# Swin block on one core: the copied values in two buffers in turn, unit 0's statistics ahead of other weights, and a new order of the pieces

## The chip, the cores and the metric

The kernel runs on one core of one Trainium2 chip. The metric is the device time of one execution in microseconds (us); the figure given for a kernel is the median of several executions.

## The reference, cut to what matters

The input `x` is [16, 192, 56, 56] in float32. One Swin block is computed on it and added to it:

```
xl  = layernorm(x over channels) * w + b, rolled by (-3, -3), cut in 7x7 windows (49 tokens each)
q, k, v = xw @ qkv_w.T + qkv_b                     # 6 heads of 32
out = softmax(q k^T / sqrt(32)) v, @ proj_w.T + proj_b
xl  = layernorm(out, windows put back and rolled back) * w + b
h   = gelu(xl @ fc1_w.T + fc1_b)                   # 768 wide
y   = h @ fc2_w.T + fc2_b + x
```

## The kernel before, in words

One unit of work is a row of 8 windows (7 image rows, 392 tokens). There are 16 x 8 = 128 units. Every large product is made in fp32r with operands split into a high and a low part: `five` and `five_tokens` issue five products where one would be enough for a coarser result.

Every engine has a program written out by hand, `step(t, k, it)`, run for t = 0 to 134. In a step an engine runs its pieces for several units at once; `units(t)` gives them, and `u[3]` is the unit t - 3. The order of the pieces inside `step` is fixed when the kernel is written, and each engine runs its pieces strictly in that order, each with its own semaphore waits. So an engine that waits in one piece holds up all pieces behind it.

A unit goes through these pieces:

- SyncE's queue (SP): `load_groups` (x in groups of 32 channels, for the statistics), `load` (x itself), `stats_out` (mean and 1/deviation to DRAM, L395), `stats_in` (them back, spread to all partitions, L402), `spread` (L434 to L442: the values `vs` copied into the block form `vbd`, 8 DMAs per unit, 4 for each half), `store`.
- VectorE (DVE): `token_blocks` (L933), `stats` and `mean_var` of the first norm, `less_mean` and `times_rstd` (L941, L945), `lo_part` (the low parts), `v_out` (L1042 to L1047, values from PSUM to `vs`, in two halves), `row_max`, `less_max`, `row_sum`, `row_scale` of the softmax, `stats`, `mean_var`, `normalise` of the second norm, `hidden_lo` (L1004), `finish_main` (L1009) and `finish_rest` (L1017).
- ScalarE (ACT): `hi_part` (the high parts), `q_out`, `k_out`, `q_rest_out`, `k_rest_out`, `exps`, `pt_copy` (transposed probabilities out of PSUM), `gelu_hi`, `gelu_full`, `y_low`.
- GpSimd (POOL): `rstd`, `less_mean_rest` (L1182), `times_rstd_rest` (L1186), `scaled_probs` (L1198), `hidden_lo_last`, `residual`.
- TensorE (PE): `qkv` (three tiles), `values` (four pieces; they make v), `scores`, `probs_t` (transposes), `weighted` (probabilities times values, 24 products that the trace shows as 48), `project`, `x2_channels`, `fc1` (six tiles), `fc2_hi` and `fc2_lo` (six each).

PSUM has 8 banks. `BANK_USES` says which bank each piece writes and in which order the uses of a bank follow each other; `claim` makes PE wait until the last reader of the use before is done. `fc2_hi(., 0)` claims the two banks of fc2, and so waits for `finish_main` and `finish_rest` of the unit before.

There is one buffer `vs` and one buffer `vbd`. `spread(u, .)` waits for `weighted(u - 1)`, which reads `vbd`:

```
sp.wait_ge(s_vs, nth(u, 2, c))
if u > 0:
    sp.wait_ge(s_pe["o"], nth(u - 1, 1, 0))
```

and `v_out(u, .)` waits until all 8 copies of unit u - 1 have landed, since they read `vs`. In DVE's order `v_out(u, 0)` stands ahead of `finish_rest`.

At the start, SP issues the x and weight loads of L387 to L430, then `load(0, 2)` to `load(0, 6)`, and only then enters its loop, whose first `stats_out` and `stats_in` belong to unit 0. PE makes the products for the folded bias of fc1 (L506, L507) before its first step. `less_mean(0)` on DVE is preceded by `first_weights` (scaling and splitting the qkv weights), and `lo_part("x1", 0, 1)` is followed by `other_weights`.

Of the kernel before, what the change touches and what calls it, by code (L numbers as in the profile page):

```python
# [56 lines left out]
REST = 16 * (6 + 4 + MT)  # L57
# [3 lines left out]
BANK_USES = [("o", 0, 2, 2), ("o", 1, 1, 2), ("qkv", 4, 7, 0), ("fc1", 0, 0, 3), ("vt", 0, 3, 0),  # L61
# [38 lines left out]
def swin_block_program(nc, x, n1w, n1b, qkv_wt, qkv_b, proj_wt, proj_b, n2w, n2b,  # L100
                       fc1_wt, fc1_b, fc2_wt, fc2_b, out):
    ctx = ExitStack()
    with ctx:
# [65 lines left out]
        vbd = sb("vbd", [128, 2, PAIRS, 3, WP])  # L169
        vs = sb("vs", [TP, PAIRS, C])  # L170
# [59 lines left out]
        s_vbd = sem("vbd_ready")  # L230
# [141 lines left out]
        def _(sp):  # L372
# [50 lines left out]
            for vec, cols in ((n2w, 4), (n2b, 6)):  # L423
                norm_vector(sp, vec, cols, s_rest)
# [7 lines left out]
            def spread(u, c):  # L432

                sp.wait_ge(s_vs, nth(u, 2, c))  # L434
                if u > 0:
                    sp.wait_ge(s_pe["o"], nth(u - 1, 1, 0))
                src = vs[:, 2 * c:2 * c + 2, :].rearrange("p j (a e d) -> p (j a) e d", a=3, e=2)
                dst = vbd[:, :, 2 * c:2 * c + 2, :, :].rearrange("p i j a d -> p i (j a) d")
                for wi in range(2):
                    for e in range(2):  # L440
                        sp.dma_start(dst[WP * e:WP * e + N, wi, :, DH * e:DH * e + DH],  # L441
                                     src[N * wi:N * wi + N, :, e, :]).then_inc(s_vbd, 16)  # L442

            for i in range(2, AHEAD):
                load(0, i)
            for t in range(UNITS + 7):
                if t < UNITS:
                    if t > 1:
                        load_groups(t)
                if 0 <= t - 2 < UNITS:  # L450
                    stats_in(t - 2)
                if 0 <= t - 4 < UNITS:
                    spread(t - 4, 0)
                    spread(t - 4, 1)
                if 0 <= t - 1 < UNITS:
                    stats_out(t - 1)
# [18 lines left out]
        def _(pe):  # L475
# [26 lines left out]
            pe.wait_ge(s_rest, REST)  # L502
            pe.wait_ge(s_raw[2], 16 * 3)
            for m in range(MT):
                ps = psum[:, spare_1, m:m + 1]
                nc.tensor.matmul(ps, raw_1[0][:, m * 128:(m + 1) * 128], nwb[:, 6:7], start=True, stop=False)  # L506
                last = nc.tensor.matmul(ps, raw_1[1][0:CR, m * 128:(m + 1) * 128], nwb[0:CR, 7:8], start=False, stop=True)  # L507
            last.then_inc(s_bias_mm, 1)
            pe.wait_ge(s_zero, 1)
            pe.wait_ge(s_zero_qk, 4)  # L510
            pe.wait_ge(s_split, 1)

# [63 lines left out]
            def weighted(u, j):  # L576
                if j == 0:
                    claim(u, [("o", 0), ("o", 1)], (s_vbd, VMOVES, VMOVES - 1), (s_ptc, PAIRS, 0))
# [4 lines left out]
                for wi, p in ((0, 0), (0, 1), (1, 0), (1, 1), (0, 2), (1, 2)):  # L583
# [7 lines left out]
                    last = nc.tensor.matmul(ps, vbd[0:KP, wi, j, p, :], pt[:, j, block, N * side:N * side + N],  # L591
# [18 lines left out]
            def step(t, k, it):  # L610
                u = units(t)
                if u[2] is not None:
                    weighted(u[2], 0)
                    weighted(u[2], 1)
                    weighted(u[2], 2)
                    weighted(u[2], 3)
                if u[4] is not None:
                    fc2_lo(u[4], 3)
                    fc2_hi(u[4], 4)
                    fc2_hi(u[4], 5)  # L620
                    fc2_lo(u[4], 4)
                if u[0] is not None:
                    qkv(u[0], 4)
                if u[4] is not None:
                    fc2_lo(u[4], 5)
                if u[3] is not None:
                    fc1(u[3], 0)
                if u[0] is not None:
                    values(u[0], 0)
                    values(u[0], 1)  # L630
                if u[3] is not None:
                    fc1(u[3], 1)
                if u[2] is not None:
                    project(u[2], 0)
                if u[3] is not None:
                    fc1(u[3], 2)
                if u[2] is not None:
                    project(u[2], 1)
                    project(u[2], 2)
                    project(u[2], 3)  # L640
                if u[3] is not None:
                    fc2_hi(u[3], 0)
                    fc2_hi(u[3], 1)
                if u[0] is not None:
                    qkv(u[0], 3)
                if u[3] is not None:
# [606 lines left out]
```

## Time and profile before

| | |
|---|---|
| median of 3 runs | 3142.04 us (3140.3 to 3142.78) |
| the profiled execution | 3141.32 us |
| its span, first to last instruction | 3139.5 us |
| PE busy | 2916.0 us (93%) |
| ACT busy | 2679.8 us (85%) |
| DVE busy | 2641.6 us (84%) |
| POOL busy | 1298.8 us (41%) |
| granted TensorE clock, mean | 0.996 |

Busy time of an engine is the time in which at least one of its instructions runs. The shares are averages over the whole span, and what bounds a stretch is read from the waits in it. The chain of waits follows what ended last backwards, step by step, to what released it.

### The profile page before, as it was taken

To read this page: it belongs to the slowest core of one execution; us is meant where nothing else is said; L and a number is where in the kernel's file an instruction comes from. 1 tells how busy PE (TensorE), PEld (TensorE's weight loads), DVE (VectorE), ACT (ScalarE), POOL (GpSimd) and SP (SyncE) were. 2 spreads that over 40 slices of the span, in tenths; PEclk is the share of its full clock that TensorE was granted. 3 is DMA by queue.
4 is the path that set the end of the run, shared out by engine and by line. 5 is a ranking of instruction groups with operands and counts; after the bars stand their busy time and mean duration, and the time that the engine had idled before them with its cause. 6 is when DMAs were issued, how large, how long until landed. Compare 5 with 4: busy or idle time off the path is not lost.

```text
span 3139.5 us, 74916 instructions
## 1 busy us (share of the span) xinstructions
PE 2916.0 (93%) x26284; PEld 2826.4 (90%) x26284; DVE 2641.6 (84%) x7212; ACT 2679.8 (85%) x5500; POOL 1298.8 (41%) x1548
## 2 busy tenths in 40 slices
PE   3899999999999999999999999999999999999998
PEld 2899999999999999999999999999998999999998
DVE  5888888888888888888888888888888888888885
ACT  1788888888888888888888888888888888888886
POOL 1444444434444444344444434434443443444442
PEclk9999999999999999999999999999999999999999
DMA  4222322333232233323323323332322333233221
GB/s 96 55 66 67 76 66 65 75 68 67 68 75 66 65 71 72 67 67 75 67 65 73 70 65 71 72 67 67 76 66 64 71 72 66 66 72 71 65 55 28
DMA packets 606164, 213.11 MB, mean 68 GB/s; under 512 B 461411, under 2 KB 589156, under 8 KB 605796
## 3 DMA queue, kind: packets, MB, share of 16 engines
q1 hardware_dynamic: 602468, 206.64, 29.4%
q8 instruction: 217, 3.56, 0.5%
q10 hardware_dynamic: 3328, 1.68, 0.2%
q14 instruction: 151, 1.24, 0.1%
HBM read 130.69 MB, written 38.94 MB: 54 GB/s over the span
## 4 chain that ended last, share of the span: by engine, by line
PE 57%; SPq 24%; DMA 9%; DVE 5%; issue 4%; ACT 0%; POOL 0%; POOLq 0%; ACTq 0%
SPq L441 23%; DMA vbd<-vs 9%; PE psum L591 6%; PE psum L566 6%; PE psum L572 4%; PE psum L546 4%; PE psum L317 4%; PE psum L319 4%; PE psum L318 4%; PE psum L320 4%; PE psum L321 4%; PE psum L547 3%; PE psum L548 3%; PE psum L567 3%; PE psum L557 2%
## 5 line engine op out<-in xcount | busy, mean ns | idle before, releaser
L1198 POOL TENSOR_TENSOR pr<-pr,rc 98x294 f32<-98x294 f32 x512 | 346.7, 686 | 1103.2 <-DVE rc L1040 1103.2
L742 ACT ACTIVATE hh<-psum,b 128x392 fp32r<-128x392 f32 x768 | 450.5, 587 | 47.8 <-PE psum L558 23.7
L745 ACT ACTIVATE hf<-psum,b 128x392 f32<-128x392 f32 x768 | 445.8, 581 | 6.3
L546 PE MATMUL psum<-hh,w2h 128*128 128x392 f32 x768 | 274.6, 358 | 153.1 <-DVE yr L1017 153.1
L1047 DVE COPY vs<-psum 98x384 f32<-98x384 f32 x256 | 142.8, 558 | 319.4 <-DMA vbd<-vs 263.1
L1004 DVE TENSOR_TENSOR hl<-hf,hh 128x392 fp32r<-128x392 f32 x640 | 399.0, 624 | 10.8 <-ACT hf L745 10.8
L1171 POOL TENSOR_TENSOR ve<-mv,eps 98x4 f32<-98x4 f32 x256 | 80.3, 314 | 590.1 <-DVE mv L962 590.1
L546 PEld LDWEIGHTS psum<-hh,w2h 128*128 128x128 f32 x768 | 144.4, 188 | 176.2 <-issue 170.4
L967 DVE TENSOR_SCALAR xn<-psum,mv,rs 98x192 f32<-98x192 f32 x512 | 230.0, 469 | 78.1 <-POOL rs L1175 78.1
L557 PE MATMUL psum<-hl,w2h 128*128 128x392 f32 x768 | 275.0, 358 | 0.0
L780 ACT ACTIVATE km<-psum,bk,half_k 128x392 f32<-128x392 f32 x256 | 160.2, 677 | 134.4 <-PE psum L321 134.4
L317 PE MATMUL psum<-x_h,w_mh 128*128 128x392 f32 x768 | 268.7, 350 | 0.5 <-DVE o_l L993 0.5
L547 PE MATMUL psum<-hh,w2l 128*128 128x392 f32 x768 | 262.6, 342 | 0.0
L319 PE MATMUL psum<-x_l,w_mh 128*128 128x392 f32 x768 | 262.0, 341 | 0.0
L548 PE MATMUL psum<-hh,w2r 128*128 128x392 f32 x768 | 261.6, 341 | 0.0
L318 PE MATMUL psum<-x_h,w_ml 128*128 128x392 f32 x768 | 261.4, 340 | 0.0
L566 PE MATMUL psum<-km,qm 128*98 128x98 f32 x2048 | 261.0, 249 | 0.0
L558 PE MATMUL psum<-hl,w2h 128*64 128x392 f32 x768 | 260.9, 340 | 0.0
L320 PE MATMUL psum<-x_r,w_rh 128*128 128x392 f32 x768 | 260.7, 339 | 0.0
L321 PE MATMUL psum<-x_r,w_rl 128*128 128x392 f32 x768 | 259.5, 338 | 0.0
L1027 DVE TENSOR_REDUCE mx<-psum 98x6 f32<-98x294 f32 x512 | 233.6, 456 | 10.9 <-PE psum L567 0.6
L1032 DVE TENSOR_TENSOR pr<-psum,mx 98x294 f32<-98x294 f32 x512 | 234.5, 458 | 4.2
(144 smaller groups left out, 10467.4 us busy)
## 6 DMA issues: line engine op xcount, KB each, us to landing
bc<-mean_rstd SPq DMA_DIRECT2D x128, 392.0 KB, 3.6
vbd<-vs SPq DMA_DIRECT2D x1024, 36.8 KB
xg<-in_x SPq DMA_DIRECT2D x368, 96.0 KB, 2.4
xt<-in_x SPq DMA_DIRECT2D x112, 194.5 KB, 2.7
out<-xt SPq DMA_DIRECT2D x112, 194.5 KB, 1.9
xt<-in_x SPq DMA_DIRECT2D x112, 97.2 KB, 2.5
out<-xt SPq DMA_DIRECT2D x112, 97.2 KB, 2.1
xg<-in_x SPq DMA_DIRECT2D x128, 3.8 KB, 2.0
```

The costliest lines, as they stand in the source:

```text
L317: nc.tensor.matmul(ps, wmh[:, c0:c0 + m], xh, start=True, stop=False)
L318: nc.tensor.matmul(ps, wml[:, c0:c0 + m], xh, start=False, stop=False)
L319: nc.tensor.matmul(ps, wmh[:, c0:c0 + m], xl, start=False, stop=False)
L320: nc.tensor.matmul(ps, wrh[:, c0:c0 + m], xrr, start=False, stop=False)
L321: return nc.tensor.matmul(ps, wrl[:, c0:c0 + m], xrr, start=False, stop=True)
L441: sp.dma_start(dst[WP * e:WP * e + N, wi, :, DH * e:DH * e + DH], src[N * wi:N * wi + N, :, e, :]).then_inc(s_vbd, 16)
L546: nc.tensor.matmul(ym, w2h[:, m, 0:CM], hh[:, b, :], start=a, stop=False)
L547: nc.tensor.matmul(ym, w2l[:, m, :], hh[:, b, :], start=False, stop=False)
L566: nc.tensor.matmul(ps[:, TP * wi:TP * wi + TP], qm[:, w, :], km[:, w, :], start=True, stop=True)
L742: nc.scalar.activation(hh[:, m % HB, :], bank("fc1", m)[:, 0:T], ACT.Gelu, bias=b1[:, m:m + 1]).then_inc(s_hh, 1)
L745: nc.scalar.activation(hf[:, m % HB, :], bank("fc1", m)[:, 0:T], ACT.Gelu, bias=b1[:, m:m + 1]).then_inc(s_gelu, 1)
L1004: nc.vector.tensor_tensor(hl[:, b, :], hf[:, b, :], hh[:, b, :].bitcast(F32), ALU.subtract).then_inc(s_hl, 1)
```

## The change

1. `vs` and `vbd` get a second copy, used by unit parity, and `s_vbd` becomes two semaphores. `spread(u, .)` now waits for `weighted(u - 2)`, and `v_out(u, .)` for the copies of unit u - 2. PE's wait for `vbd` counts on the semaphore of its parity.
2. SP's order. In the prologue: `stats_out(0)` and `stats_in(0)` stand behind `load_groups(1)`, then come `load_groups(2)`, `load(0, 1)` and the other weights; `load(0, 2)` to `load(0, 6)` move into the loop, one per step. In the loop the second half of a unit's spread is issued one step behind its first half, and ahead of the next unit's first half.
3. The vectors of the second norm are loaded from ACT's queue (semaphore `s_n2`). The products of fc1's bias move from ahead of PE's first step to behind `qkv(0, 4)`, and DVE adds them at the end of `other_weights`. The memset of `vbd` moves from DVE to POOL.
4. `BANK_USES` is new, and so is the order in every engine's `step`.

```
-        vbd = sb("vbd", [128, 2, PAIRS, 3, WP])
-        vs = sb("vs", [TP, PAIRS, C])
+        vbd = sb("vbd", [128, 2, 2, PAIRS, 3, WP])
+        vs = sb("vs", [TP, 2, PAIRS, C])
...
             load_groups(0)
-            load(0, 0)
             for at, c0, m in qkv_columns():
                 sp.dma_start(raw_q[0][:, at:at + m], qkv_wt[0:CM, c0:c0 + m]).then_inc(s_raw[0], 16)
+            load(0, 0)
             load_groups(1)
+            stats_out(0)
+            stats_in(0)
+            load_groups(2)
             load(0, 1)
...
                 sp.wait_ge(s_vs, nth(u, 2, c))
-                if u > 0:
-                    sp.wait_ge(s_pe["o"], nth(u - 1, 1, 0))
+                if u > 1:
+
+                    sp.wait_ge(s_pe["o"], nth(u - 2, 1, 0))
...
-            for i in range(2, AHEAD):
-                load(0, i)
             for t in range(UNITS + 7):
                 if t < UNITS:
-                    if t > 1:
+                    if t > 2:
                         load_groups(t)
+                    if 1 < t < AHEAD:
+                        load(0, t)
                 if 0 <= t - 2 < UNITS:
-                    stats_in(t - 2)
+                    if t - 2 > 0:
+                        stats_in(t - 2)
                 if 0 <= t - 4 < UNITS:
-                    spread(t - 4, 0)
                     spread(t - 4, 1)
+                if 0 <= t - 3 < UNITS:
+                    spread(t - 3, 0)
                 if 0 <= t - 1 < UNITS:
-                    stats_out(t - 1)
+                    if t - 1 > 0:
+                        stats_out(t - 1)
...
             def v_out(u, c):
-                if not (isinstance(u, int) and u == 0):
-
-                    dve.wait_ge(s_vbd, nth(u - 1, VMOVES, VMOVES - 1))
+                if u > 1:
+
+                    dve.wait_ge(s_vbd[u % 2], nth(u // 2 - 1, VMOVES, VMOVES - 1))
...
+BANK_USES = [("vt", 0, 5, 0), ("qkv", 4, 7, 0), ("vt", 1, 6, 0), ("fc1", 0, 4, 3), ("fc1", 1, 1, 3),
+             ("qkv", 3, 2, 0), ("ln2", 0, 6, 2), ("ln2", 1, 0, 2), ("fc1", 2, 5, 3), ("pt", 0, 1, 1),
+             ("qkv", 2, 4, 0), ("fc1", 3, 7, 3), ("fc2", 0, 1, 3), ("fc2", 1, 3, 3), ("fc1", 4, 2, 3),
+             ("fc1", 5, 5, 3), ("s", 0, 6, 0), ("pt", 1, 7, 1), ("pt", 2, 4, 1), ("s", 1, 0, 0),
+             ("x2", 0, 2, 2), ("s", 2, 7, 0), ("x2", 1, 6, 2), ("pt", 3, 5, 1), ("s", 3, 4, 0),
+             ("o", 0, 2, 1), ("o", 1, 0, 1)]
```

The new orders, written with u for the unit of which PE makes q, k and v in its step (the other engines' step numbers are translated to PE's; a bare number is the piece's index):

- PE: values u 0; fc2_lo u-4 3; qkv u 4; fc2_lo u-4 4, 5; values u 1, 2; fc1 u-3 0; values u 3; fc1 u-3 1; qkv u 3; project u-2 0, 1, 2; fc1 u-3 2; project u-2 3; probs_t u-1 0; qkv u 2; fc1 u-3 3; fc2_hi u-3 0, 1; fc2_lo u-3 0; fc2_hi u-3 2; fc1 u-3 4; fc2_lo u-3 1, 2; fc1 u-3 5; fc2_hi u-3 3; scores u 0; probs_t u-1 1, 2; scores u 1; x2_channels u-2 0; fc2_hi u-3 4, 5; scores u 2; x2_channels u-2 1; probs_t u-1 3; scores u 3; weighted u-1 0 to 3.
- ACT: gelu_full u-4 4; gelu_hi u-4 5; pt_copy u-2 1; hi x1 u 1; pt_copy u-2 2; hi x2 u-3 0; gelu_full u-4 5; exps u-1 0; pt_copy u-2 3; hi x2 u-3 1; exps u-1 1; hi o u-2 0; exps u-1 2; hi o u-2 1; q_rest u; exps u-1 3; gelu_hi u-3 0; y_low u-4; gelu_full u-3 0; gelu_hi u-3 1; k_rest u 0; gelu_full u-3 1; k_rest u 1; k_out u 0; pt_copy u-1 0; k_out u 1; gelu_hi and gelu_full u-3 2; q_out u 0; gelu_hi and gelu_full u-3 3; q_out u 1; hi x1 u+1 0; gelu_hi u-3 4.
- DVE: less_max u-1 2; row_sum u-1 0; mean_var first norm u+2 0; row_max u-1 3; row_sum u-1 1; row_scale u-1 0; mean_var u+2 1; x2_rest_lo u-3; mean_var u+2 2; less_max u-1 3; lo o u-2; finish_main u-4; mean_var u+2 3; v_out u 0; o_rest_lo u-2; v_out u 1; token_blocks u+3; stats second norm u-2 0; stats first norm u+3 0; finish_rest u-4; stats u-2 1; row_sum u-1 2; stats u-2 2; less_mean u+1; hidden_lo u-3 0; stats u-2 3; row_scale u-1 1; mean_var u-2 0 to 2; row_scale u-1 2; mean_var u-2 3; times_rstd u+1; hidden_lo u-3 1, 2; stats u+3 1; row_sum u-1 3; normalise u-2 0, 1; stats u+3 2; normalise u-2 2, 3; row_scale u-1 3; lo x1 u+1 0; row_max u 0; hidden_lo u-3 3; less_max u 0; row_max u 1; lo x2 u-2 0; less_max u 1; hidden_lo u-3 4; lo x1 u+1 1; row_max u 2; stats u+3 3.
- POOL: scaled_probs u-2 3; hidden_lo_last u-4; scaled_probs u-1 0; rstd first norm u+2; less_mean_rest and times_rstd_rest u+1; rstd second norm u-2; scaled_probs u-1 1; residual u-4; scaled_probs u-1 2.

## Rows read from the trace of the kernel before

**Rows 1.** The page: busy time of the engines, and shares of the chain.
```profile
PE 2916.0 (93%) x26284; PEld 2826.4 (90%) x26284; DVE 2641.6 (84%) x7212; ACT 2679.8 (85%) x5500; POOL 1298.8 (41%) x1548
...
PE 57%; SPq 24%; DMA 9%; DVE 5%; issue 4%; ACT 0%; POOL 0%; POOLq 0%; ACTq 0%
```

**Rows 2.** Waits, 200 to 3000 us: total us, times, longest.
```profile
DVE vs L1047 <- DMA vbd<-vs: 236.0, 117, 4.0
...
PE psum L546 <- DVE yr L1017: 144.4, 117, 3.2
```

**Rows 3.** Chain of waits in order of time: start, us, what.
```profile
1490.46 1.56 PE psum L591 x48
1492.08 0.88 SPq L441
...
1498.02 2.22 DMA vbd<-vs
...
1501.75 0.42 PE psum L546
```

**Rows 4.** Single lines of DVE, 200 to 2900 us: min/median/max ns, first and last start.
```profile
L945 DVE TENSOR_TENSOR ym<-ym,bc x113: 511/518/524, 216.7 to 2887.1; 128x392 f32<-128x392 f32 x113
...
L1004 DVE TENSOR_TENSOR hl<-hf,hh x566: 526/557/1241, 202.4 to 2896.5; 128x392 fp32r<-128x392 f32 x189
```

**Rows 5.** Busy time of one period: length, PE, PEld, DVE, ACT, POOL.
```profile
1490.39:1514.08 23.69, 22.57 (x207) 21.90 (x206) 20.44 (x57) 21.00 (x44) 10.13 (x12) 1.00 0.34 78
```

**Rows 6.** Timeline of PE in that period: start, duration, what.
```profile
1498.13 0.25 PE L331 MATMUL psum<-wp_rl,o_b 128*98 128x192 f32 x1
1498.22 0.36 PE L317 MATMUL psum<-x_h,w_mh 128*128 128x392 f32 x1
1498.42 0.34 PE L318 MATMUL psum<-x_h,w_ml 128*128 128x392 f32 x1
1498.60 0.34 PE L319 MATMUL psum<-x_l,w_mh 128*128 128x392 f32 x1
...
1512.96 0.51 PE L566 MATMUL psum<-km,qm 128*98 128x98 f32 x4
...
1513.48 0.50 PE L530 MATMUL psum<-ident,xn 98*128 98x98 f32 x4
...
1514.08 1.61 PE L591 MATMUL psum<-pt,vbd 113*64 113x49 f32 x48
1515.61 0.45 PE L557 MATMUL psum<-hl,w2h 128*128 128x392 f32 x1
1515.90 0.34 PE L558 MATMUL psum<-hl,w2h 128*64 128x392 f32 x1
```

**Rows 7.** Timeline of the first 100 us, SP, POOL, DVE and PE.
```profile
9.49 3.20 SPq L387 DMA_DIRECT2D xg<-in_x  x5
...
38.19 0.57 SPq L395 DMA_DIRECT2D mean_rstd<-mv  x1
...
12.09 1.03 POOL L1175 TENSOR_TENSOR mv<-ve,half 98x4 f32<-98x4 f32 x1
...
42.59 1.53 DVE L933 STREAM_TRANSPOSE xtok<-xg 128x768 f32<-128x768 f32 x1 [2.36 <-DMA xg<-in_x]
44.06 0.37 DVE L898 MEMSET half_k<- 32x1 f32 x4
...
49.89 0.56 DVE L941 TENSOR_TENSOR ym<-xt,bc 128x392 f32<-128x392 f32 x1
...
53.54 0.67 PE L317 MATMUL psum<-x_h,wq_mh 128*128 128x392 f32 x1 [18.86 <-DVE x_r L996]
...
96.36 0.42 PE L317 MATMUL psum<-x_h,wq_mh 128*128 128x392 f32 x1 [3.25 <-DVE vs L1047]
```

**Rows 8.** Timeline of SP in one period, its first store to `stats_in`.
```profile
1504.27 0.38 SPq L409 DMA_DIRECT2D out<-xt  x1
...
1511.77 0.62 SPq L402 DMA_DIRECT2D bc<-mean_rstd  x1
```

More of the change, by code:

```diff
@@ L611, in step @@
                 u = units(t)
[L612 to L616, printed above, removed]
+                if u[0] is not None:
+                    values(u[0], 0)
                 if u[4] is not None:
                     fc2_lo(u[4], 3)
-                    fc2_hi(u[4], 4)
-                    fc2_hi(u[4], 5)
-                    fc2_lo(u[4], 4)
                 if u[0] is not None:
@@ L624, in step @@
                 if u[4] is not None:
+                    fc2_lo(u[4], 4)
                     fc2_lo(u[4], 5)
+                if u[0] is not None:
+                    values(u[0], 1)
+                    values(u[0], 2)
                 if u[3] is not None:
@@ L637, in step @@
                 if u[2] is not None:
-                    project(u[2], 1)
-                    project(u[2], 2)
                     project(u[2], 3)
[L641 to L646, printed above, removed]
-                    fc2_lo(u[3], 0)
-                    fc1(u[3], 3)
-                    fc2_hi(u[3], 2)
+                if u[1] is not None:
+                    probs_t(u[1], 0)
                 if u[0] is not None:
@@ L652, in step @@
                 if u[3] is not None:
+                    fc1(u[3], 3)
+                    fc2_hi(u[3], 0)
+                    fc2_hi(u[3], 1)
+                    fc2_lo(u[3], 0)
+                    fc2_hi(u[3], 2)
                     fc1(u[3], 4)
@@ L670, in step @@
                     scores(u[0], 1)
+                if u[2] is not None:
+                    x2_channels(u[2], 0)
+                if u[3] is not None:
+                    fc2_hi(u[3], 4)
+                    fc2_hi(u[3], 5)
+                if u[0] is not None:
+                    scores(u[0], 2)
+                if u[2] is not None:
+                    x2_channels(u[2], 1)
                 if u[1] is not None:
@@ L796, in step @@
                 u = units(t)
+                if u[5] is not None:
+                    gelu_full(u[5], 4)
+                    gelu_hi(u[5], 5)
+                if u[3] is not None:
+                    pt_copy(u[3], 1)
+                if u[1] is not None:
+                    hi_part("x1", u[1], 1)
+                if u[3] is not None:
+                    pt_copy(u[3], 2)
+                if u[4] is not None:
+                    hi_part("x2", u[4], 0)
+                if u[5] is not None:
+                    gelu_full(u[5], 5)
@@ new lines, in step @@
+                if u[1] is not None:
+                    q_rest_out(u[1])
+                if u[2] is not None:
+                    exps(u[2], 3)
+                if u[4] is not None:
+                    gelu_hi(u[4], 0)
+                if u[5] is not None:
+                    y_low(u[5])
+                if u[4] is not None:
+                    gelu_full(u[4], 0)
+                    gelu_hi(u[4], 1)
+                if u[1] is not None:
+                    k_rest_out(u[1], 0)
+                if u[4] is not None:
+                    gelu_full(u[4], 1)
@@ new lines, in step @@
+                if u[1] is not None:
+                    k_rest_out(u[1], 1)
+                    k_out(u[1], 0)
+                if u[2] is not None:
+                    pt_copy(u[2], 0)
+                if u[1] is not None:
+                    k_out(u[1], 1)
+                if u[4] is not None:
+                    gelu_hi(u[4], 2)
+                    gelu_full(u[4], 2)
+                if u[1] is not None:
+                    q_out(u[1], 0)
+                if u[4] is not None:
+                    gelu_hi(u[4], 3)
+                    gelu_full(u[4], 3)
@@ L851, in step @@
-                if u[0] is not None:
-                    q_out(u[0], 1)
-                if u[3] is not None:
-                    gelu_full(u[3], 4)
-                    gelu_hi(u[3], 5)
+                    gelu_hi(u[4], 4)
             steps(step)
@@ L1057, in step @@
                 if u[5] is not None:
[L1058 to L1067 removed]
+                    stats(1, u[5], 0)
                 if u[0] is not None:
@@ L1071, in step @@
                     finish_rest(u[7])
+                if u[5] is not None:
+                    stats(1, u[5], 1)
+                if u[4] is not None:
+                    row_sum(u[4], 2)
+                if u[5] is not None:
+                    stats(1, u[5], 2)
+                if u[2] is not None:
+                    less_mean(u[2], (k - 2) % SLOTS)
                 if u[6] is not None:
@@ L1127, in step @@
                     row_max(u[3], 0)
-                if u[0] is not None:
-                    mean_var(0, u[0], 0)
+                if u[6] is not None:
+                    hidden_lo(u[6], 3)
                 if u[3] is not None:
```

269 lines of the change are left out of this document (113 added, 156 removed), and 5 rows, old and new, of the table BANK_USES.

## The prediction

> **What bounds the kernel now.** I read the busy shares first: PE 93%, ACT 85%, DVE 84% [rows 1]. PE leads, but 7% of the span is not PE's, and the chain of waits gives PE only 57% of the span and SP's queue 24% [rows 1]. The waits of the steady part name the place: `fc2_hi(., 0)` waits for DVE's `finish_rest` once per unit, 144.4 us in 117 times, or 1.23 us each; DVE's `v_out` waits for the copies of the unit before, 236.0 us in 117 times [rows 2]. The chain in order of time shows how the two hang together [rows 3]: `weighted` from 1490.46, the first of 8 SP copies at 1492.08, the last copy's transfer from 1498.02 for 2.22 us, then `v_out` and `finish_rest` on DVE, and PE's product at 1501.75. That is a loop: from the start of `weighted` to the stalled product 11.3 us, and from there 12.3 us of PE work to the next `weighted` (1514.08, [rows 6]).
>
> The period is 23.84 us: the first and last start of L945, 113 units, give (2887.1 - 216.7) / 112 [rows 4]. Without the stall it is 23.84 - 1.23 = 22.61 us, which agrees with PE's 22.57 us busy in one period of 23.69 us. In that period ACT is busy for 21.00 us and DVE for 20.44 us, POOL for 10.13 us [rows 5]. So a period cannot go below about 22.6 us while PE's work stays, and ACT would then be at 93%, DVE at 90%.
>
> **1. Two buffers in turn.** `spread(u)` waits for `weighted(u - 2)`, and `v_out(u)` for copies issued a whole period before. SP's 8 issues and the transfer leave the loop. SP itself stays far from full: 6.7 us of copies (the transfer of the last starts 5.9 us behind the first issue, [rows 3], and each takes 0.8) and 8.1 us from its first store to the end of `stats_in` [rows 8], in 22.6 us. What it gives, if nothing else is late: 1.23 us per unit, 144.4 us in the 117 units of [rows 2] and about 4 us in the others, 148 us in all.
>
> **2. What is late next: the new order, laid out by hand.** I place PE's pieces one after the other from the start of `values(u, 0)` = 0, at the spacing of [rows 6]: 0.178 us for a product of 392 columns (1498.42 to 1498.60), 0.09 for one of 192 (1498.13 to 1498.22), 0.52 for a scores piece (1512.96 to 1513.48), 1.53 for `weighted` (1514.08 to 1515.61). Multiplied out: 75 x 0.178 + 40 x 0.09 + 4 x 0.52 + 1.53 + 1.6 for 18 transposes = 22.2 us; the other 0.4 us of the busy 22.57 lies where the form changes. Ends of pieces: `fc2_lo 5` 2.4, `values 1` 2.9, `values 3` 4.6, `fc1 1` 5.5, `project 1` 7.3, `project 3` 9.1, `qkv 2` 10.2, `fc2_lo 0` 12.6, `fc1 5` 15.6, `scores 0` 16.6, `scores 2` 19.6, `scores 3` 20.6, `weighted` 22.2.
>
> Against these I place the other engines in their own order, each piece at the spacing of the same period, 0.15 us for each hand-over. DVE: it waits for `fc2_lo 5` until 2.55 in `finish_main`, then `v_out 0` ends at 3.7, `v_out 1` at 5.4, `token_blocks` 6.9, waits for `project 1` until 7.5, `finish_rest` 8.5, `hidden_lo 0` 10.5, `hidden_lo 2` 12.8, `normalise 3` 15.3, waits for `scores 0` until 16.8, `lo x1 1` 20.6, `row_max 2` 21.0, and back at `finish_main` after 3.5 us of pieces, at 2.3 of the next period. The layout closes on itself with 1.8 us of idle DVE time. ACT: `gelu_hi 5` and `gelu_full 4` end at 16.4, it waits for `probs_t 1` until 17.0, the table load and `exps 0` end at 20.8, `pt_copy 3` 21.2, `hi o` 2.3 (next period), `gelu_hi 0` 5.3, `gelu_full 1` 8.1, `pt_copy 0` 9.9, `gelu_hi 3` 13.2 after 0.6 us of waiting for `fc2_lo 0`, `gelu_hi 4` 15.4: it closes with 1.1 to 1.6 us idle. POOL reaches `scaled_probs 1` at 13.5 and `scaled_probs 3` at 16.1.
>
> PE's waits, each with the time it has left: `values(u, 0)` for `lo x1` 1.9 us; `project 0` for `o_rest_lo` (4.5) 1.9; its bank for `v_out 1` 1.0; `fc2_hi 0` for `finish_rest` (8.5) 2.6 and, since bank 1 is now shared, for `pt_copy 0` 1.2; `probs_t 0` for `gelu_full 1` 1.0; `probs_t 3` for `gelu_full 5` (19.2) 0.7; `weighted`'s bank for `lo x2` 1.5 and for `less_max 1` 1.1; `weighted 3` for `pt_copy 3` 0.5. None is negative. A schedule that closes at 22.6 us with all waits met means that no loop of waits is longer, so PE again has no gap. The least cover is 0.5 us, so a single queue running a little later than laid out shows. I charge 0.1 us per unit for this, 12 us (between 0 and 0.5 us, 0 to 62 us).
>
> **3. Changes of form on PE.** One from 192 to 392 columns costs 0.02 us (1498.22 to 1498.42 against 0.18), the one after `weighted` 0.11 (1515.61 to 1515.90) [rows 6]. Before there were five, at 0.19 us together; in the new order there are seven (four of the first kind, two from transposes to 392 columns, one from `weighted` to 192), for which these two rows give 0.12 to 0.41 us. The difference is -0.07 to +0.22 us per unit, -9 to +28 us; I take +6 us, near the cheap row, because five of the seven are like or near it.
>
> **4. Unit 0's statistics ahead.** Before, `stats_out(0)` is issued at 38.19 us though its data were ready at 13.1 [rows 7]. Now it follows `load_groups(1)`, which ends at 12.7 (9.49 + 3.20, and the same issues lie ahead of it). DVE is there sooner, one memset of 1.3 us less. Then 2 us to land, `stats_in`, and the three groups of unit 2 from 15.5 to 18.1 with 2.5 us to land. DVE takes `token_blocks(2)` (1.5 us) ahead of the weights, so `first_weights` starts at about 22.5 in place of 44.06, ends 5.8 us later (44.06 to 49.89) at 28.3, and PE's first product of unit 0 comes 3.65 us behind (49.89 to 53.54), at 32.0 in place of 53.54 [rows 7]: -21.5 us (between -14, if the groups of unit 2 or bc come late behind the weight loads, and -25). The products of fc1's bias, 6.2 us, now lie inside unit 0's step. DVE spends 9 us in `other_weights` at that time and PE has nothing that could pass it, so they cost nothing; uncovered they would cost 6.2. The vectors on ACT's queue end at about 21 us, ahead of ACT's first work at 28, and are free.
>
> **5. First units and the end.** Between 57 and 100 us PE waits for the same copies, 3.25 us once at 96.36 [rows 7], and other waits there are for chains of latencies that stay. I take -6 us (0 to -12). The last seven steps have the same pieces: 0 +- 3.
>
> The sum against the profiled execution: 3141.3 - 148 + 12 + 6 - 21.5 - 6 = 2983.8 us. The median shown is 0.7 us above it, so 2984 us is forecast for the median too.
>
> **A rule against the change.** L1004 takes 557 ns in the median but up to 1241 [rows 4], so some DVE operations with two SBUF inputs already stand behind a GpSimd one. The Trainium skill (SBUF - State Buffer, "SBUF: two separate sides") says that such a DVE operation and a GpSimd operation hold one port pair exclusively, whichever starts first, for its whole length. By this rule the trace's spread is a matter of who meets whom, and the new order decides it anew; it is the second rival.
>
> **Rivals.**
> A. Another engine becomes the bound. ACT and DVE have only 1.1 to 1.8 us of idle time in the layout, and each engine's waits add if they fall at other places: ACT's 21.00 us plus the 2.0 us of waits laid out gives 23.0 us, DVE's 20.44 + 0.35 + 1.8 = 22.6. At 23.2 us per unit the steady part gives only 0.64 x 120 = 77 us: 3141 - 77 - 27 + 6 = 3043 us. For it: three engines over 90% on strict queues. Against it: the waits in the layout are waits for PE, which shrink when an engine runs late. 14%.
> B. The copies' wait goes but PE's stays: the loop closes over `finish_main`, `finish_rest` and the bank shared with `pt_copy 0`, or over SP's strict order (`store(u-4)` waits for `residual` at 14.5, and `stats_in` and both spreads queue behind it). Then only the start is won: 3141 - 27 = 3114 us. Against it: SP is through with the spreads at 7.1 of the next period, 13 us before `weighted`. 5%.
> C. Slower: DVE and POOL collide. Nine DVE operations per unit read two SBUF operands (five `hidden_lo`, `less_mean`, `times_rstd`, two `lo x1`), and a collision costs up to 1241 - 557 = 0.68 us. DVE has 23.84 - 20.44 - 0.35 = 3.05 us to the old period, so from five collisions more per unit on, the kernel is slower. At seven more, DVE's period is 20.8 + 4.8 = 25.6 us: 3141 + 1.75 x 120 - 27 = 3324 us; at five, about 3160. Against it: POOL is busy for 10.1 of 22.6 us, most of it laid out beside `token_blocks`, `stats` and `normalise`. 3%.
> The change doing what it says with the waits gone has 78%.
>
> **How the numbers follow.** The likeliest case by itself reaches from 3141 - 148 - 9 - 25 - 12 = 2947 to 2984 + 50 (0.5 us per unit in place of 0.1) = 3034 us, most of it between 2955 and 3020. The range is drawn down to 2948 and up to 3050, which takes in rival A. What this measurement can tell from no change is 0.2%, about 6 us. Faster: the likeliest case, A, and all but a little of B, 0.94; within 0.2%: 0.02; slower: C and what I have not seen, 0.04.
>
> **What would show it.** Right: the wait of `v_out` for `vbd<-vs` and of L546 for `yr` gone from the waits; PE over 97% busy from 200 to 2900 us at a period of 22.6 to 22.8; the first product of unit 0 near 32 us; DVE idle in `finish_main` and before the second norm's statistics, waiting for PE. Wrong: a new wait of PE once per unit (for `pt`, `gelu_full` or `lo x1`), PE busy for more than 22.9 us per unit (step 3), L1004's mean well above 0.62 us (rival C), or `stats_out(0)` later than 15 us (step 4).

## The result and the profile after

The changed kernel takes 2939.93 us (median of 4 runs, 2938.56 to 2941.19) against 3141.17 us of the kernel before, timed beside it (3137.77 to 3142.78): a ratio of 0.9361, 95% interval 0.9344 to 0.9377. The forecast was 2984 us, in the range 2948 to 3050. The direction and the place of the gain came out as forecast; the gain is 44 us larger, and the time lies 8 us below the lower end of the range. The profiled execution took 2939.99 us, with a span of 2938.2 us and a granted clock of 0.999.

The page of the changed kernel: busy time of the engines, and the shares of the chain that ended last (against [rows 1]).

```profile
PE 2888.9 (98%) x26284; PEld 2820.7 (96%) x26284; DVE 2692.8 (92%) x7211; ACT 2689.2 (92%) x5500; POOL 1365.5 (46%) x1549
...
PE 97%; DVE 1%; ACT 1%; SPq 0%; DMA 0%; issue 0%; POOL 0%; POOLq 0%; ACTq 0%
```

SP's queue and the transfers, together a third of the chain before, are off it: the chain is PE's own work. PE's busy time also fell, by 27.1 us, with the same 26,284 products. It is the first sign of where the missing 44 us lie: if busy time were work alone, the same products would have the same busy time.

Its waits from 200 to 2900 us (total us, times, longest; against [rows 2]):

```profile
DVE mx L1046 <- PE psum L575: 122.8, 120, 2.2
...
ACT pt L713 <- PE psum L580: 62.6, 121, 0.7
...
ACT hh L756 <- PE psum L566: 32.4, 122, 1.0
...
PE psum L318 <- DVE pr L1051: 0.6, 1, 0.6
...
PE psum L580 <- ACT hf L759: 0.2, 1, 0.2
```

Both waits of [rows 2] are gone. What waits now is DVE, for the scores (1.02 us per unit; 0.8 was laid out), and ACT, for `probs_t` (0.52; 0.6 laid out) and `fc2_lo 0` (0.27; 0.6 laid out): all for PE. DVE also waits 0.21 us per unit for ACT's high part. The two other waits of DVE that were laid out, in `finish_main` and ahead of the second norm's statistics, did not come (7.6 us in 8 times in all). PE itself waits for nobody, two single waits in 120 units aside. The windows say the same (length, then busy time of PE, PEld, DVE, ACT and POOL, granted clock, DMA share, GB/s; the second is one period, against [rows 5]):

```profile
200.00:2900.00 2700.00, 2699.19 (x24658) 2639.22 (x24657) 2505.48 (x6717) 2531.56 (x5172) 1276.07 (x1440) 1.00 0.32 72
...
1517.98:1540.40 22.42, 22.42 (x207) 21.93 (x205) 20.89 (x57) 21.04 (x44) 10.65 (x13) 1.00 0.32 73
```

Single lines of DVE, min/median/max ns, first and last start (against [rows 4]):

```profile
L964 DVE TENSOR_TENSOR ym<-ym,bc x119: 532/533/539, 208.5 to 2853.5; 128x392 f32<-128x392 f32 x119
...
L1023 DVE TENSOR_TENSOR hl<-hf,hh x604: 528/558/568, 207.2 to 2899.0; 128x392 fp32r<-128x392 f32 x151
```

119 units give a period of (2853.5 - 208.5) / 118 = 22.415 us, against 23.842 before. The starts of `weighted` divide the whole difference of the spans, 3139.5 - 2938.2 = 201.3 us. First the kernel before, then the changed one, the fourth and the last but one of each:

```profile
154.86 1.61 PE L591 MATMUL psum<-pt,vbd 113*64 113x49 f32 x48
...
3086.17 1.61 PE L591 MATMUL psum<-pt,vbd 113*64 113x49 f32 x48
```

```profile
128.24 1.61 PE L600 MATMUL psum<-pt,vbd 113*64 113x49 f32 x48
...
2885.36 1.61 PE L600 MATMUL psum<-pt,vbd 113*64 113x49 f32 x48
```

Up to the first of these lie 26.6 us (154.86 - 128.24), in the 123 periods between them 123 x 1.416 = 174.2 us, and behind the last 0.5 us. The start (timeline, SP, DVE and PE; against [rows 7]):

```profile
12.74 0.47 SPq L396 DMA_DIRECT2D mean_rstd<-mv  x1
...
14.97 0.35 SPq L403 DMA_DIRECT2D bc<-mean_rstd  x1
15.36 2.73 SPq L388 DMA_DIRECT2D xg<-in_x  x5
...
25.89 1.53 DVE L952 STREAM_TRANSPOSE xtok<-xg 128x768 f32<-128x768 f32 x1 [8.18 <-DMA xg<-in_x]
...
32.07 0.56 DVE L960 TENSOR_TENSOR ym<-xt,bc 128x392 f32<-128x392 f32 x1
...
35.16 0.45 PE L328 MATMUL psum<-wq_mh,x_h 128*98 128x192 f32 x1 [16.33 <-DVE x_r L1015]
```

### The profile page after: what moved, and what is told of

Its sections match the earlier page's. It is cut to its first block, busy times and chain, and to the rows that moved or that the text cites. A ratio compares the mean times of both kernels' runs of the same rounds, so it can differ in the third digit from the quotient of the medians.

```text
span 2938.2 us, 75046 instructions
## 1 busy us (share of the span) xinstructions
PE 2888.9 (98%) x26284; PEld 2820.7 (96%) x26284; DVE 2692.8 (92%) x7211; ACT 2689.2 (92%) x5500; POOL 1365.5 (46%) x1549
## 4 chain that ended last, share of the span: by engine, by line
PE 97%; DVE 1%; ACT 1%; SPq 0%; DMA 0%; issue 0%; POOL 0%; POOLq 0%; ACTq 0%
PE psum L318 8%; PE psum L319 7%; PE psum L320 7%; PE psum L322 7%; PE psum L321 7%; PE psum L600 7%; PE psum L574 6%; PE psum L554 5%; PE psum L565 5%; PE psum L555 5%; PE psum L566 5%; PE psum L556 5%; PE psum L580 4%; PE psum L328 4%; PE psum L330 3%; PE psum L329 3%
## 5 line engine op out<-in xcount | busy, mean ns | idle before, releaser
L1215 POOL TENSOR_TENSOR pr<-pr,rc 98x294 f32<-98x294 f32 x512 | 385.9, 764 | 382.3 <-DVE rc L1059 382.3
L759 ACT ACTIVATE hf<-psum,b 128x392 f32<-128x392 f32 x768 | 451.7, 588 | 6.3
L1209 POOL TENSOR_TENSOR hl<-hf,hh 128x392 fp32r<-128x392 f32 x128 | 226.0, 1766 | 374.3 <-ACT hf L759 374.3
L1023 DVE TENSOR_TENSOR hl<-hf,hh 128x392 fp32r<-128x392 f32 x640 | 347.7, 559 | 3.8 <-ACT hf L759 3.7
L318 PE MATMUL psum<-x_h,w_mh 128*128 128x392 f32 x768 | 275.0, 358 | 0.7 <-DVE pr L1051 0.6
L713 ACT ACTIVATE pt<-psum 113x294 f32<-113x294 f32 x512 | 207.1, 405 | 70.4 <-PE psum L580 70.2
L565 PE MATMUL psum<-hl,w2h 128*128 128x392 f32 x768 | 264.5, 344 | 0.3 <-POOL hl L1209 0.3
L574 PEld LDWEIGHTS psum<-km,qm 128*98 128x98 f32 x2048 | 237.0, 166 | 11.3 <-ACT qm L716 4.6
L768 ACT ACTIVATE pr<-pr 98x294 f32<-98x294 f32 x512 | 230.2, 450 | 7.7 <-DVE pr L1051 3.1
```

The source lines that it names most:

```text
L318: nc.tensor.matmul(ps, wmh[:, c0:c0 + m], xh, start=True, stop=False)
L565: nc.tensor.matmul(ym, w2h[:, m, 0:CM], hl[:, b, :], start=False, stop=z)
L574: nc.tensor.matmul(ps[:, TP * wi:TP * wi + TP], qm[:, w, :], km[:, w, :], start=True, stop=True)
L759: nc.scalar.activation(hf[:, m % HB, :], bank("fc1", m)[:, 0:T], ACT.Gelu, bias=b1[:, m:m + 1]).then_inc(s_gelu, 1)
```

## The experiments

The first three ask where the missing gain lies. Theory 1: a wait of PE costs more than the idle time that the profile labels with it. The last product ahead of it counts as busy to its end, and in a stream without a wait that tail lies under the next products; behind the wait the first products follow each other more slowly. So PE's real floor lies below the 22.57 us of [rows 5], and taking the stall away gives more than 1.23 us. Theory 2: the stall is worth 1.23 us, and PE's work became cheaper through the new order. The other experiments take the parts of the change apart.

**One part alone: the two buffers, in the order before.**

```
-        vbd = sb("vbd", [128, 2, PAIRS, 3, WP])
-        vs = sb("vs", [TP, PAIRS, C])
+        vbd = sb("vbd", [128, 2, 2, PAIRS, 3, WP])
+        vs = sb("vs", [TP, 2, PAIRS, C])
...
-                if u > 0:
-                    sp.wait_ge(s_pe["o"], nth(u - 1, 1, 0))
+                if u > 1:
+                    sp.wait_ge(s_pe["o"], nth(u - 2, 1, 0))
...
```

> The kernel before with the two buffers alone (vs and vbd by parity, two semaphores); the order of every queue and the banks stay as before. Theory 1 (a stall of PE costs more than its labelled idle time, because the product before it drains and the one behind it refills the pipeline: 0.16 + 0.08 us per stall): the waits of v_out for the copies and of fc2_hi for finish_rest vanish and the period falls from 23.84 to about 22.4 us, 2965 to 2975 us in all. Theory 2 (a stall costs its idle time of 1.23 us, and the rest of the gain is the new order's cheaper changes of form on PE): the waits vanish but the period stays at 22.6 us, 2988 to 2996 us. Theory 3 (the new order was needed to remove the wait): a wait of PE stays each unit, above 3030 us.

Measured: 2953.45 us (2951.82 to 2954.46), ratio 0.9403 (0.9389 to 0.9417). The line that paces DVE, PE's window and DVE's wait:

```profile
L946 DVE TENSOR_TENSOR ym<-ym,bc x112: 511/516/523, 315.6 to 2798.6; 128x392 f32<-128x392 f32 x112
```

```profile
300.00:2800.00 2500.00, 2500.00 (x22927) 2438.61 (x22925) 2297.26 (x6263) 2333.71 (x4808) 1139.21 (x1339) 1.00 0.32 74
```

```profile
DVE vs L1047 <- PE psum L331: 92.1, 95, 1.0
```

The period is (2798.6 - 315.6) / 111 = 22.369 us, without a gap on PE. This is the old order, so theory 2 is out: the stall by itself was worth 23.842 - 22.369 = 1.473 us per unit, and the new order's period is 0.046 us longer than this. PE's busy time over the run fell from 2916.0 to 2883.8 us, with the same number of products. The time is also some 12 us below the lower end that theory 1 gave, mostly because the fill became shorter as well: the fourth `weighted` starts at 147.19 us instead of 154.86, 7.7 us sooner, with the first product of unit 0 where it was (53.64).

**A wait with next to nothing in it.** PE waits for its own last product once per unit, behind `fc2_lo 5`:

```
                     fc2_lo(u[4], 5)
+                    pe.wait_ge(s_pe["fc2"], nth(u[4], MT, MT - 1))
```

> The kernel after with one wait added per unit: behind fc2_lo(u-4, 5) PE waits for that product itself before it goes on to values(u, 1). Nothing is late; PE only may not overlap two products at this place. Theory 1: the hidden cost of a stall shows by itself, drain and refill, 0.2 to 0.35 us per unit, of which only 0.0 to 0.1 us is labelled as idle: 2965 to 2985 us. Theory 2: what a wait costs is its labelled idle time: below 0.1 us per unit, 2940 to 2952 us.

Measured: 2976.42 us (2975.8 to 2977.01), ratio 0.9476 (0.946 to 0.9492). DVE's pacing line, PE's window, and PE's timeline at the place:

```profile
L965 DVE TENSOR_TENSOR ym<-ym,bc x111: 532/536/539, 302.7 to 2799.0; 128x392 f32<-128x392 f32 x111
```

```profile
300.00:2800.00 2500.00, 2493.66 (x22577) 2404.89 (x22576) 2314.34 (x6176) 2318.48 (x4738) 1172.87 (x1322) 1.00 0.32 73
```

```profile
1518.74 0.33 PE L566 MATMUL psum<-hl,w2h 128*64 128x392 f32 x1
...
1519.14 0.33 PE L328 MATMUL psum<-wq_mh,x_h 128*98 128x192 f32 x1
1519.31 0.25 PE L329 MATMUL psum<-wq_ml,x_h 128*98 128x192 f32 x1
```

The same three products in the changed kernel without the wait:

```profile
1521.88 0.33 PE L566 MATMUL psum<-hl,w2h 128*64 128x392 f32 x1
1522.05 0.25 PE L328 MATMUL psum<-wq_mh,x_h 128*98 128x192 f32 x1
1522.13 0.25 PE L329 MATMUL psum<-wq_ml,x_h 128*98 128x192 f32 x1
```

The period is (2799.0 - 302.7) / 110 = 22.694 us, 0.279 more than without the wait, and the window counts as idle only (2500 - 2493.66) / 110 = 0.058 us of it. The timeline shows the rest: the next product comes 0.40 us behind the last one instead of 0.17 (1519.14 - 1518.74 against 1522.05 - 1521.88), but 0.33 us of the 0.40 count as busy. The one behind it comes after 0.17 instead of 0.08. Together 0.23 + 0.09 = 0.32 us, close to the 0.279.

What the slow restart is, PE's weight loads show (PEld), first in the changed kernel, then behind the wait:

```profile
1521.88 0.16 PEld L328 LDWEIGHTS psum<-wq_mh,x_h 128*98 128x98 f32 x1
```

```profile
1519.13 0.16 PEld L328 LDWEIGHTS psum<-wq_mh,x_h 128*98 128x98 f32 x1 [0.43 <-PE psum L566]
1519.22 0.17 PEld L329 LDWEIGHTS psum<-wq_ml,x_h 128*98 128x98 f32 x1
```

In the stream a product's weights are loaded 0.17 us ahead of it, under the product before (1521.88 for 1522.05). Behind the wait the first load starts together with its product (1519.13 and 1519.14), and the second product follows its own load, which starts 0.09 us later. So the wait also takes away the lead of the weight loads.

**Four such waits** (also behind `values 1`, `qkv 3` and `project 1`).

```
+                    pe.wait_ge(s_pe["vt"], nth(u[0], 2, 0))
...
+                    pe.wait_ge(s_pe["qkv"], nth(u[0], 3, 1))
...
+                    pe.wait_ge(s_pe["ln2"], nth(u[2], 2, 0))
```

> The kernel after with four waits of PE for its own last product per unit: behind fc2_lo(u-4, 5), values(u, 1), qkv(u, 3) and project(u-2, 1). One such wait cost 36.5 us in all, 0.28 us per unit, 0.06 of it labelled idle. Theory 1 (each place where products may not overlap costs about the same, drain and refill): 3 more times 0.2 to 0.28 us per unit, period 23.3 to 23.55 us, 3050 to 3085 us. Theory 2 (the first wait cost its 0.28 because it moved other engines into PE's way): much less than proportional, below 3020 us.

Measured: 3086.74 us (3086.0 to 3087.31), ratio 0.9834 (0.9819 to 0.9849).

```profile
L968 DVE TENSOR_TENSOR ym<-ym,bc x106: 532/535/539, 309.9 to 2786.5; 128x392 f32<-128x392 f32 x106
```

```profile
300.00:2800.00 2500.00, 2475.68 (x21730) 2321.25 (x21730) 2223.62 (x5936) 2242.66 (x4559) 1126.94 (x1272) 1.00 0.31 70
```

The period is (2786.5 - 309.9) / 105 = 23.587 us: 1.172 more, 0.293 for each wait, of which 0.058 is counted as idle (24.3 us in some 105 units, by four). The period and the time lie just above the upper ends of theory 1 (23.55 us and 3085 us), so the cost adds up, by a little more than in proportion. Four waits for nothing cost four fifths of what the removed stall cost, with a fifth of its labelled idle time.

**The new order with one buffer.** The inverse of the first edit on the changed kernel, and both halves of the copies issued together, as before:

```
+                    spread(t - 4, 0)
                     spread(t - 4, 1)
...
-                if 0 <= t - 3 < UNITS:
-                    spread(t - 3, 0)
```

> The kernel after with one buffer of vs and vbd and both halves of the spread issued together as before; all else as after. Theory: the loop comes back and the new order makes it worse, since v_out(u, 0) waits for copies that start with the period: 8 issues and a landing end at 8.9 us, v_out 1 about 5.7 us later than laid out, and project 0 shares its bank: 4 to 5 us of PE stall per unit, 3450 to 3550 us. Rival (the order alone gives the gain, the buffers little): within 50 us of the kernel after, below 2990 us.

Measured: 3866.11 us (3864.3 to 3870.85), ratio 1.2312 (1.2293 to 1.233), granted clock 0.903. The waits, and PE behind one of them:

```profile
DVE vs L1065 <- DMA vbd<-vs: 435.6, 84, 6.9
PE psum L328 <- DVE vs L1065: 421.5, 84, 6.8
```

```profile
1503.74 0.30 PE L328 MATMUL psum<-wp_mh,o_h 128*98 128x192 f32 x1 [4.15 <-DVE vs L1065]
...
1506.36 0.53 PE L319 MATMUL psum<-x_h,w_ml 128*128 128x392 f32 x1
1506.69 0.53 PE L320 MATMUL psum<-x_l,w_mh 128*128 128x392 f32 x1
```

```profile
1500.00:1510.00 10.00, 6.26 (x38) 6.27 (x39) 6.93 (x17) 4.61 (x11) 0.71 (x1) 0.83 0.05 7
```

The loop of [rows 3] is back, and dearer: PE waits 421.5 / 84 = 5.0 us per unit (300 to 2800 us), as the expectation had it. Its reason, that the new order asks for `v_out` earlier behind `weighted`, was not tested apart. The time was missed by over 300 us, because the expectation knew only the wait. Behind it the products of 392 columns last 0.53 us and follow each other after 0.33, about half the speed of the other runs. The granted clock is at its lower level of 1.2 GHz there: PE had stood still for 4.15 us up to 1503.74, the clock's mean is 0.53 from 1504 to 1506 us and 0.61 from 1506 to 1508, and from 1508 on it is 1.00 again (0.83 in the mean of these 10 us). The period is 29.84 us, 7.4 more than with two buffers. How the 2.4 us that are not labelled wait divide was not measured apart; if such a stall hides 0.24 us, as the one of the kernel before does, some 2.1 us are the clock's, an estimate.

**The start put back** (SP's prologue as before, the rest as changed).

```
-            stats_out(0)
-            stats_in(0)
-            load_groups(2)
...
+            for i in range(2, AHEAD):
+                load(0, i)
```

> The kernel after with SP's prologue as before: stats_out(0) and stats_in(0) in the loop, behind load(0, 2) to load(0, 6). Theory: the start term is real and not given back: first product of unit 0 about 18 us later, 2956 to 2963 us in all. Rival (the delay is absorbed in the fill, since units 1 to 3 wait for chains of latencies anyway): less than 10 us, below 2950 us.

Measured: 2957.38 us (2957.31 to 2957.94), ratio 0.9417 (0.9402 to 0.9431): 17.5 us slower than the changed kernel.

```profile
50.47 0.45 PE L328 MATMUL psum<-wq_mh,x_h 128*98 128x192 f32 x1 [31.71 <-DVE x_r L1010]
```

PE starts 50.47 - 35.16 = 15.3 us later, not 18, and 17.5 us are lost, 16.3 of them ahead of the fourth `weighted` (144.56 against 128.24). The start is a term of its own.

**Both terms without the new order** (two buffers and the new start, PE's, DVE's and ACT's order and the banks as before).

> The kernel before with the two buffers and the new start (SP's prologue, second-norm vectors on ACT's queue, fc1's bias products behind qkv(0, 4), vbd's memset on POOL), but the old banks, the old order of pieces and both halves of the spread together. Theory (the two terms add, and the new order is worth nothing or costs 5 us): 2953 less 18, 2933 to 2938 us, so a little below the kernel after (2940). Rival (the new order is needed for the early start, since the old one has v_out and token_blocks of later units in the way of unit 0): 2945 us or more.

Measured: 2935.86 us (2934.87 to 2937.61), ratio 0.9354 (0.934 to 0.9368), 17.6 us below the buffers alone. The terms add: the fourth `weighted` starts at 129.01 us, 18.2 sooner than with the buffers alone. The new order of the pieces gave nothing: the changed kernel's 2939.93 us lie 4 us above, in line with its longer period (0.046 x 123 = 5.7 us).

**The order of one piece.** `lo_part("x1", u[2], 1)` moved behind `row_max(u[3], 2)` and `stats(0, u[0], 3)`, away from POOL's `hidden_lo_last`.

> The kernel after with DVE's lo_part(x1, u+1, 1) moved behind row_max(u, 2) and stats(u+3, 3), away from POOL's hidden_lo_last. Theory (the two have two SBUF inputs and block each other; it costs DVE and POOL time but not the kernel's): the DVE piece falls from 1283 to about 560 ns and POOL's from 1777 to 1030 to 1300 ns, total within 3 us of the kernel after. Rival (the long durations have another cause, such as operands waiting in the engine): both stay above 1200 ns. A PE wait at values(u, 0) would show that the 1.9 us of cover laid out there were needed.

Measured: 2939.18 us (2938.41 to 2940.3), ratio 0.9364 (0.935 to 0.938). The groups from 200 us on (busy us, mean ns | idle before), first in the changed kernel, then here:

```profile
L1015 DVE TENSOR_TENSOR x_r<-yr,x_r 64x392 fp32r<-64x392 f32 x119 | 152.6, 1283 | 3.8
...
L1209 POOL TENSOR_TENSOR hl<-hf,hh 128x392 fp32r<-128x392 f32 x120 | 213.2, 1777 | 349.5 <-ACT hf L759 349.5
```

```profile
L1015 DVE TENSOR_TENSOR x_r<-yr,x_r 64x392 fp32r<-64x392 f32 x119 | 76.1, 639 | 3.7
...
L1209 POOL TENSOR_TENSOR hl<-hf,hh 128x392 fp32r<-128x392 f32 x120 | 212.4, 1770 | 348.6 <-ACT hf L759 348.6
```

DVE's collision costs 0.64 us per unit and can be taken away, and nothing follows, since DVE has 1.02 us of waiting for PE. POOL's operation, which I had expected to fall as well, stays as long. The edit took only one of two DVE operations away from it: `hidden_lo`, which has two SBUF operands as well, starts 0.33 us behind POOL's operation in both versions (1516.96 and 1516.63 there, 1517.47 and 1517.14 here). So what was moved is not what lengthens it; `hidden_lo` may be, and was not tested.

**PE's first product sooner.** In front of DVE's step 2, on the version with the old order (`b_best`), there with `stats_out(1)` behind `load(0, 1)` as well (`b_best2`), and on the changed kernel (`a_first`):

```
+                if t == 2:
+                    less_mean(0, 0)
+                    times_rstd(0)
...
-                if u[2] is not None:
+                if u[2] is not None and t > 2:
                     less_mean(u[2], (k - 2) % SLOTS)
...
```

`b_best` is this edit alone on the old order:

> As b_two_stats, and in DVE's step 2 first_weights, less_mean(0) and times_rstd(0) stand at the front, ahead of token_blocks(2), where DVE idles for 8.2 us in the kernel after (17.7 to 25.9 us). Theory: unit 0's x1 is ready 5 to 7 us sooner and all of it reaches the end, 2926 to 2931 us. Rival (the other weights and the loads for them become the bound of the fill): less than 3 us below b_two_stats.

`b_best2` adds the earlier `stats_out(1)`, since DVE stood 3.59 us for it in `b_best`:

> The old order with two buffers, the new start, the pieces of unit 0 at the front of DVE's step 2, and stats_out(1) issued behind load(0, 1), ahead of the other weights. Theory (DVE's wait of 3.6 us for stats_out(1) held the first product): it comes at 30 to 31 us in place of 33.9 and the total is 3 to 4 us less, 2931 to 2933 us, the lowest of all. Rival (units 1 and 2 are held by DVE's other_weights and the loads behind it): 2934 to 2936 us.

> The kernel after with first_weights, less_mean(0) and times_rstd(0) at the front of DVE's step 2. In the old order the same edit brought 1.4 us at the first product, because DVE then waited 3.6 us for stats_out(1) in a mean_var piece that stands ahead of lo_part(x1, 0, 1). In the new order that piece comes one step later. Theory: the first product of unit 0 comes 4 to 6 us sooner (29 to 31 us) and the total falls by as much, 2934 to 2937 us. Rival (other_weights then waits for the loads of fc1's bias that SP issues until 28.7 us, and the fill gives it back): less than 2 us below the kernel after.

Measured: `b_best` 2935.56 us (2935.3 to 2935.86), ratio 0.9353 (0.9337 to 0.9369); `b_best2` 2932.19 us (2930.38 to 2932.81), 0.9331 (0.9319 to 0.9344); `a_first` 2939.34 us (2937.51 to 2939.59), 0.9354 (0.9341 to 0.9366). Timelines of the start, in this order:

```profile
32.93 0.25 DVE L974 BATCH_NORM_AGGREGATE mv<-st 98x2 f32<-98x6 f32 x2 [3.59 <-DMA mean_rstd<-mv]
...
33.91 0.66 PE L318 MATMUL psum<-x_h,wq_mh 128*128 128x392 f32 x1 [15.06 <-DVE x_r L1008]
```

```profile
29.90 0.66 PE L318 MATMUL psum<-x_h,wq_mh 128*128 128x392 f32 x1 [11.02 <-DVE x_r L1009]
```

```profile
29.53 0.45 PE L328 MATMUL psum<-wq_mh,x_h 128*98 128x192 f32 x1 [10.82 <-DVE x_r L1015]
...
31.78 0.28 DVE L930 CAST pb_hi<-pb 1x256 fp32r<-1x256 f32 x1 [2.40 <-DMA b<-in_fc_b]
...
49.58 0.33 PE L328 MATMUL psum<-wq_mh,x_h 128*98 128x192 f32 x1 [2.10 <-DVE x_r L1015]
```

`b_best` missed its 2926 to 2931 us and lies 0.3 us below the version without the edit, where its rival put it: the first product came 1.4 us sooner (33.91 against 35.27), not 5 to 7. `a_first` missed too, and its rival was right as well. PE starts 5.6 us sooner than in the changed kernel, but DVE stands for a load, and PE for the next unit's norm at 49.58; at the fourth `weighted` 2.2 us are left (126.06 against 128.24), and at the end 0.6, which is within the runs' spread. `b_best2` came as its theory said. It starts as early as `a_first` and keeps it: at the fourth `weighted` it is 3.4 us ahead of `b_best` (124.28 against 127.70) and the same at the end. It is the fastest version, 7.2 us below `a_first` on the same chip, with ranges that don't touch, and faster than both kernels of this change, with the order and the banks of the old one. Only 1.8 of these 7.2 us lie ahead of the fourth `weighted`; the rest is the shorter period of the old order.

## Why the forecast was right in kind and 44 us too high

**Step 1, the stall, is the one that failed, by its size.** That the copies' loop sets the period and that two buffers end it was right: both waits are gone, here and with the buffers alone. But the step took the stall at its labelled 1.23 us and named 22.57 us busy as PE's floor. The buffers alone show 1.473 us per unit. The 0.24 us between, over the 123 periods 30 us, stood in the busy time. The lower end of the range took the stall at its label too (148 us), which is why the time could fall below it. The prediction's own sum held a sign of it: multiplied out, PE's products came to 22.2 us, and the other 0.4 of the 22.57 were put on changes of form, for which step 3 found only 0.19; 22.2 + 0.19 is within 0.03 of the 22.369 measured. The rows of the kernel before let the rest be seen, ahead of and behind the stall:

```profile
1500.38 0.25 PE L331 MATMUL psum<-wp_rl,o_b 128*98 128x192 f32 x1
...
1501.75 0.42 PE L546 MATMUL psum<-hh,w2h 128*128 128x392 f32 x1 [1.12 <-DVE yr L1017]
1502.01 0.34 PE L547 MATMUL psum<-hh,w2l 128*128 128x392 f32 x1
```

The product at 1500.38 lasts 0.25 us, of which in a stream 0.09 would be its own before the next starts ([rows 6], 1498.13 to 1498.22): 0.16 us of tail that only a stall lays bare. The first product behind the stall takes 0.26 us to the next instead of 0.18: another 0.08. Together 0.24 us, what the buffers alone gave beyond the label, and what a self-wait costs beyond its label: 0.279 or 0.293 less 0.058, 0.22 to 0.24 us.

The Trainium skill (TensorE: Matmul & The Clock Gate, "Single matmul latency" and "Back-to-back issue gap") gives the latency of a product of N columns as (398 + N) / 2.4 ns and the isolated gap between two as N / 2.4 + 2.5 ns, for bf16 products at the full clock. For 392 columns that is 0.33 and 0.166 us, where the rows here, of fp32r products, have 0.33 to 0.34 and 0.17 to 0.18. For a stream with weight loads the page has a shorter spacing, about 131 ns at 512 columns, which no row here comes near. The tail is the difference of duration and spacing; that it is part of the price of a wait, the self-waits show.

**Step 2, the layout,** was right in what it was for: no wait of PE per unit. The largest waits of DVE and ACT are where it put them, 1.02 and 0.52 us where 0.8 and 0.6 were laid out; DVE's two smaller ones, in `finish_main` and ahead of the second norm's statistics, which were named as a sign of being right, did not show. The 12 us charged for a queue running late were not due: PE waits 0.8 us in 2700. With step 1 this is 42 of the 44 us: a period of 22.76 us was forecast (23.84 - 1.23 + 0.1 + 0.05), 22.415 measured, 0.345 x 123.

**Step 3, the changes of form,** came out at its size: +0.05 us per unit was taken, +0.046 is the difference of two gapless kernels (22.415 and 22.369). It is all that the new order does to PE's period; that it comes from the changes of form was not tested apart.

**Steps 4 and 5, start and fill,** were forecast at -21.5 and -6 us. The first product comes 53.54 - 35.16 = 18.4 us sooner, and 26.6 us lie ahead of the fourth `weighted`, of which the buffers alone give 7.7. That the sum comes so close to 27.5 is partly luck: the start gave 3 us less than forecast, and what follows it nearly 3 us more. `stats_out(0)` (12.74) and `stats_in` (14.97) came as laid out, at 12.7 and 15. What was off: the groups of unit 2, issued until 18.1, let DVE wait 8.18 us and `token_blocks(2)` start at 25.89 instead of 21, since the last of them landed some 7.8 us after its issue and not 2.5. Weights and x were being loaded at the same time, the likely reason, not tested. That case was in the bound (-14 if they come late). `first_weights` then took 4.3 us in place of 5.8 and gave a part back.

**The rivals.** A, another engine as the bound, did not come: DVE and ACT are at 93 and 94% of the steady window, and nearly all of their waits are for PE. B, PE still waiting, is out by the same rows. C, collisions, was right that the order decides who meets whom, and near in the price of one (0.68 us; 1283 - 560 = 0.72 here), but it needed five more of them per unit to cost time. `hidden_lo` fell from a mean of 624 to 558 ns, while `lo x1 1` rose from 560 to 1283 and `hidden_lo_last` on POOL from 1032 to 1777. One period, from DVE's and POOL's timeline of the changed kernel:

```profile
1516.96 0.56 DVE L1023 TENSOR_TENSOR hl<-hf,hh 128x392 fp32r<-128x392 f32 x1
...
1517.55 1.28 DVE L1015 TENSOR_TENSOR x_r<-yr,x_r 64x392 fp32r<-64x392 f32 x1
...
1516.63 1.78 POOL L1209 TENSOR_TENSOR hl<-hf,hh 128x392 fp32r<-128x392 f32 x1 [2.90 <-ACT hf L759]
```

DVE's operation from 1517.55 holds out until POOL's has ended at 1518.41, and 0.42 us longer. The rule that the prediction names from the Trainium skill (SBUF - State Buffer, "SBUF: two separate sides") fits it. It does not fit the operation ahead of it as the rows stand, which starts 0.33 us after POOL's and keeps its 0.56 us, while POOL's is the one that grows. The profile's spans on POOL are rough, so it stays open whether POOL's operation held the ports by then. In all DVE's busy time rose by some 0.4 us per unit, under its 1.02 us of waiting.

## What to carry to other kernels

When the bounding engine is a pipelined one, price a stall at its labelled idle time plus the difference of a product's duration and its spacing (0.16 us here) plus the slow restart (0.08), here 0.24 us on 1.23. And take that engine's floor from its spacing times its counts, since its busy time holds one such tail per wait. Take away first the wait that ends last, and test it alone before the work behind it is placed anew: here the buffers alone gave 188 of the 201 us, the earlier start 18, and the new order took some 4 back. An earlier first product is worth only what the second and third units can follow.

## What the runs showed of the hardware that I had not expected

- A wait of PE for its own last product costs 0.28 us (0.293 each with four), of which 0.058 us show as idle. Behind it the weight loads have lost their lead of 0.17 us on the products.
- A wait of some 5 us in each unit brought the granted clock down: 0.903 over the run, products of 392 columns at 0.33 us spacing behind the wait instead of 0.18. Waits of 1.2 us in each unit of the kernel before had left it at full speed (1.00 from 200 to 2900 us).
- The 5 loads for unit 2's statistics took 5.1 to 8.6 us from issue to landing while weights and x were being loaded; the median over the run is 2.4.
- Where a DVE and a POOL operation with two SBUF operands meet, either can be the one that grows: POOL's from 1032 to 1777 ns with the first DVE operation at full speed, DVE's next from 560 to 1283. With the second moved away POOL's stays at 1770, and the first still starts 0.33 us behind it. What lengthens it was not taken apart.
